# A gap of 128 instead of 64 bytes ahead of four SBUF tiles: y_hi, y_lo, hid_hi and hid_lo

## The chip, the cores and the metric

One Trainium2 chip, one core in use. The time is the device time of one launch in microseconds (us), and the metric is the median of the runs. Engines are named as in the profile: PE is TensorE's matmuls, PEld its weight loads, ACT ScalarE, DVE VectorE, POOL GpSimd, SP the queue that issues the DMAs.

## What is computed

A block of two sub-layers over x of shape (8, 1024, 256) in float32, each behind a layer norm and a residual addition:

```
# first sub-layer, x normalized, D=256, inner width 512, state 16
xz = x @ w_in;  xp, z = split(xz)
xc = silu(causal_conv4(xp) + conv_b)
h  = 0.9*h + 0.1*(xc_t @ w_B);  ys_t = h @ w_C        # scan over the sequence
x  = x + (ys * silu(z)) @ w_out
# second sub-layer, x normalized; 2 of 8 experts for each sequence, by its first token
h  = gelu(x @ W1[e] + b1[e]);   o = h @ W2[e] + b2[e]
x  = x + (o of expert 1 + o of expert 2) / 2
```

## The kernel before

The work goes by chunks of 512 tokens: 16 chunks, two for each sequence. The matmuls take float32r operands. For precision every product A·B is made of three: each operand is split into a high part and the rest (`..._hi`, `..._lo`), and hi·hi, hi·lo and lo·hi are added up in PSUM. ScalarE writes the high parts, VectorE or GpSimd the low parts.

The two operands that this change is about are stationary ones. `y_hi` and `y_lo` hold the gated output ys·silu(z), `hid_hi` and `hid_lo` the GELU rows; all four are [128, 4, 512] in float32, 8192 bytes in each partition. In `tokens` (L1311 to L1313; for the last half chunk `down_tile`, L1320 to L1322) a block of 128 of their columns is loaded as weights, and 256 columns of `w_out_hi`/`w_out_lo` or `w2_hi`/`w2_lo` stream through it:

```
mm(dst, his[:, j, rows], whi, ...)      # L1311
mm(dst, his[:, j, rows], wlo, ...)      # L1312
mm(dst, los[:, j, rows], whi, ...)      # L1313
```

`out_proj` makes 48 of these matmuls for a chunk, `down` another 48. All other products (`project`, L1202 to L1207, for the in-projection and the experts' first layer; `state_in`, L1351 and L1354; `state_out`, L1373) load 128 columns of a weight matrix and stream 512 columns of tokens.

Each engine runs a program written out by hand, with semaphores between them. A step s works on three chunks at once: TensorE makes `xp` of chunk s, `out_proj` of chunk s-1, `z` of chunk s, `up` of chunk s-2, `state_in` of s, half and more of `down` of s-2, `state_out` of s, and the rest of `down`. A step has 84 matmuls of 512 columns and 96 of 256 columns. Steps 4 to 13 are a loop of pairs; an even step also chooses the experts of a sequence. `state_out` waits for VectorE's `state_lo` (L793, tile `state_mix`), which in VectorE's program stands behind `hidden_lo` (L793, tile `hid_lo`) and the scan (L958).

Tiles lie in SBUF in the order in which they are declared, each rounded up to 32 bytes. In this order the padding tiles `to_line`, `wb_rest` and `behind_columns` set the places. From `ident` on, every tile ahead of `behind_columns` starts at a multiple of 512 bytes in its partition, all other operands of matmuls among them, but for the small ones of the router (`first_tok`, `w_router`, `w_spread`). `behind_columns` is read and written by nothing; it is 64 bytes long, so the four tiles behind it start 64 bytes past a multiple of 512. Every block of weights that is loaded from them starts at the same place, since `rows` steps by 512 bytes and `j` by 2048.

Of the kernel before, what the change touches and what calls it, by code (L numbers as in the profile page):

```python
# [11 lines left out]
P = 128  # L12
# [9 lines left out]
def build_block(nc, x, w_in, conv_w, conv_b, w_B, w_C, w_out, Wr, br, W1, b1, W2, b2, out):  # L22
# [19 lines left out]
    with ExitStack() as ctx:  # L42
        def sb(name, shape, dt=F32):
            return ctx.enter_context(nc.sbuf_tensor(name, shape, dt))
# [48 lines left out]
        w1_hi, w1_lo = sb("w1_hi", [P, TOP_K, KD * D], F32R), sb("w1_lo", [P, TOP_K, KD * D], F32R)  # L93
        b_mix = sb("b_mix", [P, JD, P], F32R)
        c_mix = sb("c_mix", [P, DI], F32R)
        behind_columns = sb("behind_columns", [P, 16])
        y_hi, y_lo = sb("y_hi", [P, JD, CH], F32R), sb("y_lo", [P, JD, CH], F32R)
        hid_hi, hid_lo = sb("hid_hi", [P, JF, CH], F32R), sb("hid_lo", [P, JF, CH], F32R)

# [1404 lines left out]
```

## Time and profile before

| | us |
|---|---|
| median of 3 runs | 520.37 |
| the three runs | 520.37, 517.02, 520.53 |
| the profiled execution, its own time | 517.04 |
| its span, first to last instruction | 515.2 |
| PE busy in the span | 508.1 |
| DVE busy | 454.0 |
| ACT busy | 400.0 |
| POOL busy | 342.7 |

The span and all rows come from the one profiled execution; 1.8 us of its own time lie outside the span. Busy is the time in which at least one instruction of the engine runs. Matmuls overlap: each has a duration of some 280 or 390 ns in the profile, and the next starts before it ends, so the pace of TensorE is read from the distance of the starts, not from the durations.

### The profile page before, as it was taken

The numbers are of one execution on the slowest core, as the hardware profiler recorded it, in microseconds if no ns is written. First come the engines' busy times: TensorE is split into PE (matmuls) and PEld (weight loads), VectorE is DVE, ScalarE is ACT, GpSimd is POOL, SyncE is SP. The second block draws the span as 40 slices with busy tenths as digits, with TensorE's granted clock in tenths as the row PEclk, the third lists the DMA queues.
The fourth block names the chain that finished last, engine by engine and source line by source line (L and its number), as shares of the span: only waits on it lengthen the run. The fifth ranks groups of instructions, "written<-read, shape, count | busy, mean of one in ns | idle before, by whom it ended". The sixth has DMA issues, their size and how long they took to land.

```text
span 515.2 us, 9745 instructions
## 1 busy us (share of the span) xinstructions
PE 508.1 (99%) x3008; PEld 447.3 (87%) x3008; DVE 454.0 (88%) x901; ACT 400.0 (78%) x690; POOL 342.7 (67%) x368
## 2 busy tenths in 40 slices
PE   8999999999999999999999999999999999999997
PEld 7788798889898898988889898888988889898987
DVE  5999999999998899989999899998999979896773
ACT  3975877887878788697886979779788787969444
POOL 4764656929875496937969199681996639773381
PEclk9999999999999999999999999999999999999999
DMA  8960104426143352504325161442604333130102
GB/s 247 289 224 1 41 1 144 143 80 208 43 157 89 125 162 78 182 25 166 119 99 186 41 200 45 142 143 68 218 14 149 122 123 122 49 116 0 43 2 81
DMA packets 53922, 57.79 MB, mean 112 GB/s; under 512 B 8714, under 2 KB 50186, under 8 KB 53770
## 3 DMA queue, kind: packets, MB, share of 16 engines
q1 hardware_dynamic: 52042, 57.19, 33.5%
q10 hardware_dynamic: 1856, 0.31, 0.3%
q8 instruction: 12, 0.20, 0.2%
q14 instruction: 12, 0.10, 0.1%
HBM read 35.98 MB, written 21.50 MB: 112 GB/s over the span
## 4 chain that ended last, share of the span: by engine, by line
PE 55%; DVE 14%; issue 9%; ACT 4%; DVEq 0%; POOL 0%; ACTq 0%
PE blk L1202 9%; PE blk L1203 9%; PE blk L1207 9%; PE tok L1311 7%; PE tok L1313 7%; PE tok L1312 7%; DVE hid_lo L793 3%; DVE conv L909 3%; PE blk L1373 3%; PE turn L1351 1%; PE turn L1354 1%; DVE stats_t L830 1%; DVE stats_t L804 1%; DVE normed L892 1%; DVE xn_lo L793 1%
## 5 line engine op out<-in xcount | busy, mean ns | idle before, releaser
L456 POOL TENSOR_TENSOR y_lo<-gate,y_hi 128x512 fp32r<-128x512 f32 x55 | 70.2, 1306 | 105.5 <-ACT y_hi L556 105.5
L909 DVE SCALAR_TENSOR_TENSOR conv<-blk,tap_w,conv 128x512 f32<-128x512 f32 x192 | 130.1, 740 | 11.1 <-ACT conv L618 11.0
L1202 PE MATMUL blk<-xn_hi,w_in_hi 128*128 128x512 f32 x232 | 91.2, 393 | 0.6 <-ACT xn_hi L556 0.6
L1203 PE MATMUL blk<-xn_hi,w_in_lo 128*128 128x512 f32 x232 | 90.6, 391 | 0.0
L421 POOL TENSOR_TENSOR xc_lo<-conv,xc_hi 128x512 fp32r<-128x512 f32 x59 | 71.0, 1221 | 10.5 <-ACT xc_hi L556 10.3
L1311 PE MATMUL tok<-w_out_hi,y_hi 128*128 128x256 f32 x256 | 72.3, 282 | 0.6 <-DVE y_lo L793 0.3
L1207 PE MATMUL blk<-xn_lo,w_in_hi 128*128 128x512 f32 x232 | 72.0, 391 | 0.1
L1313 PE MATMUL tok<-w_out_hi,y_lo 128*128 128x256 f32 x256 | 71.8, 280 | 0.0
L1312 PE MATMUL tok<-w_out_lo,y_hi 128*128 128x256 f32 x256 | 71.8, 280 | 0.0
L618 ACT ACTIVATE conv<-blk,tap_b,tap_w 128x512 f32<-128x512 f32 x64 | 49.1, 778 | 28.3 <-PE blk L1207 24.8
L1311 PE MATMUL tok<-w_hi,hid_hi 128*128 128x256 f32 x248 | 70.2, 283 | 0.3 <-DVE hid_lo L793 0.3
L1313 PE MATMUL tok<-w_hi,hid_lo 128*128 128x256 f32 x248 | 69.6, 281 | 0.0
L1312 PE MATMUL tok<-w_lo,hid_hi 128*128 128x256 f32 x248 | 69.5, 280 | 0.0
L793 DVE TENSOR_TENSOR hid_lo<-hid,hid_hi 128x512 fp32r<-128x512 f32 x64 | 50.8, 820 | 18.4 <-ACT hid_hi L556 18.3
L624 ACT ACTIVATE conv<-conv 128x512 f32<-128x512 f32 x64 | 39.2, 631 | 33.6 <-DVE conv L909 32.6
L464 POOL TENSOR_TENSOR x_mid<-x_mid,b_sel 128x256 f32<-128x256 f32 x60 | 50.8, 882 | 3.2 <-DVE hid_lo L793 1.3
L1207 PEld LDWEIGHTS blk<-xn_lo,w_in_hi 128*128 128x128 f32 x232 | 43.5, 188 | 10.3 <-DVE xn_lo L793 1.1
L1202 PEld LDWEIGHTS blk<-xn_hi,w_in_hi 128*128 128x128 f32 x232 | 43.5, 188 | 9.2 <-DVE w_in_lo L793 0.8
L1203 PEld LDWEIGHTS blk<-xn_hi,w_in_lo 128*128 128x128 f32 x232 | 43.6, 188 | 8.2
L1311 PEld LDWEIGHTS tok<-w_out_hi,y_hi 128*128 128x128 f32 x256 | 48.1, 188 | 1.9 <-issue 0.7
L1312 PEld LDWEIGHTS tok<-w_out_lo,y_hi 128*128 128x128 f32 x256 | 48.9, 191 | 0.5
L1312 PEld LDWEIGHTS tok<-w_lo,hid_hi 128*128 128x128 f32 x248 | 47.4, 191 | 1.1
(175 smaller groups left out, 1300.5 us busy)
## 6 DMA issues: line engine op xcount, KB each, us to landing
spill<-normed SPq DMA_DIRECT2D x25, 512.0 KB, 2.8
normed<-spill SPq DMA_DIRECT2D x100, 128.0 KB, 2.8
x_mid<-in_L_attn_x SPq DMA_DIRECT2D x30, 256.0 KB, 2.7
out<-x_mid SPq DMA_DIRECT2D x30, 256.0 KB, 2.5
x_in<-in_L_attn_x SPq DMA_DIRECT2D x14, 512.0 KB, 3.9
w_all<-in_L_ffn_W SPq DMA_DIRECT2D x2, 2048.0 KB, 12.0
b_all<-in_L_ffn_b SPq DMA_DIRECT2D x1, 1024.0 KB, 14.6
gate<-in_L_attn_w_in SPq DMA_DIRECT2D x2, 256.0 KB, 4.6
```

The costliest lines, as they stand in the source:

```text
L421: nc.gpsimd.tensor_tensor(xc_lo[:, j, :], conv[:, j, 0:CH], xc_hi[:, j, :].bitcast(F32), ALU.subtract).then_inc(xc_lo_set, 1)
L456: nc.gpsimd.tensor_tensor(y_lo[:, j, :], gate_of(o, j), y_hi[:, j, :].bitcast(F32), ALU.subtract).then_inc(y_lo_set, 1)
L464: ins = nc.gpsimd.tensor_tensor(mid(f, q)[:, n, :], mid(f, q)[:, n, :], b2_sel[:], ALU.add)
L618: nc.scalar.activation(conv[:, j, HALO:HALO + CH], blk[j][:], ACT.Identity, bias=tap_b[:, j:j + 1], scale=tap_w[:, j, 0:1]).then_inc(tap_f ...
L793: return nc.vector.tensor_tensor(dst, src, hi.bitcast(F32), ALU.subtract)
L909: nc.vector.scalar_tensor_tensor(cols, blk[j][:], tap_w[:, j, t:t + 1], cols, ALU.mult, ALU.add).then_inc(tap_added, 1)
L1202: mm(dst, whi(k), his(k), start=(k == 0), stop=False)
L1203: mm(dst, wlo(k), his(k), start=False, stop=False)
L1207: ins = mm(dst, whi(k), los(k), start=False, stop=(k == KD - 1))
L1311: mm(dst, his[:, j, rows], whi, start=(j == 0 and n == 0), stop=False, skip_group_check=True)
L1312: mm(dst, his[:, j, rows], wlo, start=False, stop=False, skip_group_check=True)
L1313: ins = mm(dst, los[:, j, rows], whi, start=False, stop=(last and n == 1), skip_group_check=True)
```

## The change

The padding tile doubles, from 16 to 32 float32 elements in each partition. The four tiles behind it move up by 64 bytes, to 128 bytes past a multiple of 512. No instruction is added, removed or reordered.

```diff
         b_mix = sb("b_mix", [P, JD, P], F32R)
         c_mix = sb("c_mix", [P, DI], F32R)
-        behind_columns = sb("behind_columns", [P, 16])
+        behind_columns = sb("behind_columns", [P, 32])
         y_hi, y_lo = sb("y_hi", [P, JD, CH], F32R), sb("y_lo", [P, JD, CH], F32R)
         hid_hi, hid_lo = sb("hid_hi", [P, JF, CH], F32R), sb("hid_lo", [P, JF, CH], F32R)
```

## Rows read from the trace of the kernel before

**Rows 1.** The page: busy time, and TensorE's granted clock in 40 slices.

```profile
PE 508.1 (99%) x3008; PEld 447.3 (87%) x3008; DVE 454.0 (88%) x901; ACT 400.0 (78%) x690; POOL 342.7 (67%) x368
PEclk9999999999999999999999999999999999999999
```

**Rows 2.** Busy time of each engine by stretches of one step (length, busy, instructions).

```profile
118.40:149.20 30.80, 30.61 (x181) 27.00 (x180) 29.11 (x54) 25.82 (x45) 25.68 (x27) 1.00 0.36 120
149.20:180.00 30.80, 30.80 (x186) 27.28 (x185) 27.06 (x58) 24.69 (x41) 18.04 (x20) 1.00 0.37 121
...
sum 154.00, PE 153.66 PEld 135.93 DVE 141.76 ACT 126.88 POOL 113.20; mean PE 30.73 PEld 27.18 DVE 28.35 ACT 25.38 POOL 22.64
```

**Rows 3.** All waits of PEld between 118 and 420 us.

```profile
PEld blk L1373 <- DVE state_mix L793: 1.5, 5, 0.4
```

**Rows 4.** Timeline of PE, a stretch of 48 in step 4, first four and last.

```profile
118.42 0.28 PE L1311 MATMUL tok<-w_out_hi,y_hi 128*128 128x256 f32 x1
118.54 0.28 PE L1312 MATMUL tok<-w_out_lo,y_hi 128*128 128x256 f32 x1
118.66 0.28 PE L1313 MATMUL tok<-w_out_hi,y_lo 128*128 128x256 f32 x1
118.78 0.28 PE L1311 MATMUL tok<-w_out_hi,y_hi 128*128 128x256 f32 x1
...
123.96 0.28 PE L1313 MATMUL tok<-w_out_hi,y_lo 128*128 128x256 f32 x1
124.08 0.40 PE L1202 MATMUL blk<-xn_hi,w_in_hi 128*128 128x512 f32 x1
```

**Rows 5.** Timeline of PE, the first stretch of 48, after a wait.

```profile
43.61 0.36 PE L1311 MATMUL tok<-w_out_hi,y_hi 128*128 128x256 f32 x1 [0.34 <-DVE y_lo L793]
...
44.38 0.28 PE L1311 MATMUL tok<-w_out_hi,y_hi 128*128 128x256 f32 x1
...
49.03 0.28 PE L1313 MATMUL tok<-w_out_hi,y_lo 128*128 128x256 f32 x1
```

**Rows 6.** One line's loads and matmuls: duration in ns, min/median/max.

```profile
L1312 PEld LDWEIGHTS tok<-w_out_lo,y_hi x256: 187/192/192, 43.7 to 488.2; 128*128 128x128 f32 x128
L1312 PEld LDWEIGHTS tok<-w_lo,hid_hi x248: 187/192/192, 74.2 to 509.3; 128*128 128x128 f32 x124
L1311 PEld LDWEIGHTS tok<-w_out_hi,y_hi x256: 186/188/192, 43.6 to 488.1; 128*128 128x128 f32 x128
```

**Rows 7.** Timeline of PE, `project` later in the same step.

```profile
125.46 0.39 PE L1202 MATMUL blk<-xn_hi,w_in_hi 128*128 128x512 f32 x1
...
126.82 0.39 PE L1202 MATMUL blk<-xn_hi,w_in_hi 128*128 128x512 f32 x1
```

**Rows 8.** Timeline of PE around `state_out` in step 4.

```profile
140.99 0.28 PE L1313 MATMUL tok<-w_hi,hid_lo 128*128 128x256 f32 x1
141.46 1.21 PE L1373 MATMUL blk<-state_mix,c_mix 128*128 128x512 f32 x4 [0.19 <-DVE state_mix L793]
```

**Rows 9.** All waits of DVE for others between 190 and 440 us, the longest.

```profile
DVE hid_lo L793 <- ACT hid_hi L556: 6.0, 12, 0.6
DVE conv L909 <- ACT conv L618: 5.9, 16, 0.6
DVE state_mix L793 <- ACT state_mix L556: 4.6, 8, 0.6
```

**Rows 10.** One line each of ACT, DVE and POOL: duration in ns, min/median/max.

```profile
L556 ACT ACTIVATE y_hi<-gate x60: 622/632/639, 39.1 to 482.3; 128x512 fp32r<-128x512 f32 x60
L556 ACT ACTIVATE state_mix<-state x16: 632/632/639, 34.1 to 477.1; 128x512 fp32r<-128x512 f32 x16
L793 DVE TENSOR_TENSOR hid_lo<-hid,hid_hi x64: 644/693/1411, 69.4 to 508.1; 128x512 fp32r<-128x512 f32 x64
L793 DVE TENSOR_TENSOR xn_lo<-normed,xn_hi x50: 676/692/1712, 95.0 to 465.4; 128x512 fp32r<-128x512 f32 x50
L456 POOL TENSOR_TENSOR y_lo<-gate,y_hi x55: 1285/1295/1827, 39.8 to 481.2; 128x512 fp32r<-128x512 f32 x55
L421 POOL TENSOR_TENSOR xc_lo<-conv,xc_hi x59: 1077/1287/1564, 21.9 to 467.0; 128x512 fp32r<-128x512 f32 x59
```

## The prediction

> **What bounds the kernel now.** I read the page first. TensorE is busy 508.1 of 515.2 us, VectorE 454.0, and the clock is at its upper level in every slice [rows 1]. So the clock can neither be lost nor won by a change that moves no work. The table by steps says the same of the inside: of a step of 30.8 us TensorE is busy 30.6 to 30.8, VectorE 29.1 in an even and 27.1 in an odd step [rows 2]. The list of waits has just one kind for the weight loads in ten steps, on VectorE's `state_mix`: 1.5 us in five places [rows 3]. TensorE is the bound, and what one of its instructions loses or gains is seen in the time, but VectorE is close behind in every second step.
>
> A busy engine isn't one at its best pace, so next comes the distance of the starts. This is the view on which everything below rests. In step 4 the 48 matmuls of `out_proj` start from 118.42 to 123.96 us: 5.54 us by 47 distances is 117.8 ns [rows 4]. In the opening the same 48 instructions follow a wait for `y_lo`, and from the seventh on (44.38 us) to the last (49.03) there are 41 distances in 4.65 us: 113.4 ns [rows 5]. Same tiles, same addresses, same clock, and 4.4 ns apart. In the slower stretch the weight load of L1312 takes longer than its neighbours: its median is 192 ns, that of L1311 188 [rows 6]. `project`, whose operands all start at multiples of 512 bytes, makes six matmuls of 512 columns in 126.82 - 125.46 = 1.36 us, 227 ns each, which is twice 113.4 [rows 7]. I read that as two floors with the same price for a column, 0.443 ns, and a surcharge of 4.4 ns for each matmul of 256 columns in most stretches.
>
> How many matmuls carry the surcharge? There are 1536 of the kind (16 chunks by 96). Counted through the timeline between the first (43.61 us) and the last (510 us) of them, 1489 distances lie within a stretch; 1276 are 117 to 119 ns, as in [rows 4], 186 are 113 to 116, as in [rows 5], and 27 are longer. All stretches that TensorE enters without a pause run at 117.8; the faster pace comes only behind a pause, and lasts to the end of the stretch. So the surcharge is 1276 by 4.4 ns = 5.6 us of the kernel.
>
> **The change part by part.** It adds and removes no instruction and moves no wait. What can change is how long an instruction takes that touches one of the four tiles. There are three kinds.
>
> *The writers and readers on ScalarE, VectorE and GpSimd.* Their tiles lie 64 bytes off now, and the trace has twins whose output lies at a multiple of 512: ScalarE 632 ns against 632, VectorE 693 against 692, GpSimd 1295 against 1287 [rows 10]. An offset of 64 costs 0 to 8 ns. For one of 128 the trace has only GpSimd's and ScalarE's source `conv`, which is no worse. Bounds: 8 ns either way by 64 on VectorE is 0.5 us, by 55 on GpSimd 0.4 us. GpSimd's part is hidden, as it is busy 113.2 of 154 us [rows 2]; VectorE's stands in the chain to `state_mix` only in even steps. I take zero, and 0.5 us for the range.
>
> *The DMAs.* None reads or writes the four tiles. Zero.
>
> *The weight loads, 1536 of them, and the matmuls beside which they run.* No row shows another offset of a weight than 0 and 64, so the cost has to be bounded by the nearest rows. Below: the surcharge goes everywhere, -5.6 us, as in [rows 5]. Further below lies only a price never seen in the trace: if 256 columns took 256 cycles at 2.4 GHz, 106.7 ns, then 11.1 ns by 1489 is -16.5 us; I give that little weight, as `project` at offset 0 doesn't reach it either [rows 7]. Above: the surcharge is 13.3 ns for a group of three, and one load of the three (L1312) shows it. If two of three carry it, the pace is 122.2 ns: 1276 by 4.4 and 186 by 8.8 is +7.2 us. If all three do, 126.6 ns: +13.7 us. That is the upper bound.
>
> Which value? The surcharge comes and goes at one and the same address, with the way in which the stretch was entered. So it isn't a price of the address itself but of how loads and matmuls fall into step, and the floor of 0.443 ns for a column is the same for weights at 0 (`project`) and at 64 (the stretch behind the wait). That speaks for a floor that an offset doesn't touch, and for a stepping that it may touch. I take 0 for the forecast, since the two offsets that the trace has, 0 and 64, share a floor. The entries to the stretches stay the same too: `project` ahead, no pause.
>
> On ports the Trainium skill ("TensorE: Matmul & The Clock Gate", step ① of "Step-by-step: what each phase is for") says that TensorE reads the streaming operand and the weights over two independent ports, so that a load takes nothing from the matmul that runs. By that rule an offset changes nothing and the sum is 0. The trace agrees only in part: the same addresses run at 113.4 and at 117.8 ns, so something between the two streams isn't independent. The same page ("Back-to-back issue gap") gives N/2.4 + 2.5 ns for isolated matmuls, an estimate of 109 ns for 256 columns; by it at most 13 us would be to be had, and no stretch of this trace gets there.
>
> *What a gain would meet.* In step 4 the stretch of `down` ahead of `state_out` ran at the faster pace in its second half and ended at 140.99 us; the next matmul started at 141.46, since `state_mix` wasn't ready [rows 8]. That is 0.47 us against 0.11, so 0.36 us of waiting, in one of two steps. VectorE in an even step is busy 29.1 of 30.8 us, and waits for ScalarE some 16.5 us in all over 250 us, 2 us a step [rows 2, 9]. So a gain in an even step is partly handed back at `state_out`. A gain of 4.4 ns by 96 is 0.42 us for a step; I let even steps keep half, odd ones all: 4.2 of the 5.6 us. A loss meets no such cushion: the waits that could take it up are 1.5 us in all [rows 3], and the loss arrives in full but for that.
>
> **The sum.** The profiled execution took 517.04 us, span 515.2. The change as I take it is 0, so a like execution would take 517.0. The median of the runs is 520.37, though, with one run at 517.02 and two near 520.5. The profiled one is at the lower of these levels, and I know no reason for the difference. An unchanged kernel would give a median at one of the two or between; I put it at 519.5.
>
> **The rivals.**
>
> *The surcharge goes (faster).* The loads fall into step with the matmuls in every stretch. For it: the pace exists in the trace with these instructions. Against: one has to believe that 64 more bytes do what a pause does now. It gives 519.5 - 4.2 = 515.3, and 519.5 - 5.6 = 513.9 if VectorE gives nothing back. By the measure of 1% (5.2 us, about what a measurement of this kernel tells from no change) this is on the edge. With luck in the floor too, it reaches 510 and less.
>
> *A second load of each three collides (slower).* Its place is the stretches of L1311 to L1313, its price 4.4 ns more for each matmul, and it decides as soon as more than one load in three is slowed: then the 1489 distances cost +7.2 us, 526.7, and with all three +13.7, 533.2. For it: one load in three does collide at 64, so the streams aren't free of each other, and TensorE has no pause in which to hide a loss. Against: `project` at offset 0 shows no lasting surcharge, so a collision isn't what an arbitrary offset brings.
>
> *The placement doesn't do anything measurable, as the two streams settle into the same pace.* This is the forecast. That the change doesn't move the tiles at all is excluded by the layout: 64 bytes more in front of the four tiles are 64 bytes for each.
>
> **How the numbers follow.** Forecast, same pace: 0.45, between 516.5 and 521. Surcharge gone: 0.25, of which a good half comes out past 1% (515.2); a lower floor: 0.05. More loads collide: 0.25, from 524 to 533, and nearly all past 1% (525.6). That gives faster 0.22, same 0.48, slower 0.30, with some weight on slower because nothing takes up a loss. The range leaves out the lower floor and the worst of the collisions, and takes in the 0.5 us for VectorE: 511.5 to 529.5. The likeliest case alone has 516.5 to 521.
>
> **What the profile of the changed kernel would show.** If the forecast holds: 48 starts of `out_proj` in 5.54 us, L1312's loads at a median of 192 ns, the waits on `state_mix` near 1.5 us in ten steps. If the surcharge is gone: 5.33 us for the 48, loads at 188, and more waiting on `state_mix` in even steps. If more collides: 5.74 us or more for the 48, loads over 188 ns in two lines or three, and no waits of PEld at all. `project` should keep 227 ns in each case, and the durations of ScalarE, VectorE and GpSimd on the four tiles should stay within 8 ns. I would be wrong in kind if `project` changed its pace, if one of the other engines' instructions did, or if the paces stayed and the time didn't.

## The result: 0.43% slower

The changed kernel takes 519.67 us, the median of 20 runs, and the kernel before 517.17 us in 20 runs. The ratio estimated from all of these runs is 1.0043, with an interval of 1.0023 to 1.0062. That is a small loss, and it is real. The median is next to the forecast of 519.5, and inside the range. But the forecast stood for "same pace, no change", counted from a median of 520.4 of three runs. Against the 517.2 of twenty runs there is a change, and the prediction didn't see it coming.

Both kernels have two levels of time. Before: 11 runs at 516.9 to 517.2 and 9 at 520.3 to 520.8. After: 12 at 519.2 to 519.8 and 8 at 522.6 to 523.3. Lower against lower, the change costs 519.4 - 517.1 = 2.3 us. The profiled execution of the changed kernel took 522.59 us, so it is one of the upper level, while that of before is one of the lower. What sets the levels is told below; rows of after are read here with that in mind.

No instruction changed its place or count, so the first view is the busy time. TensorE went from 508.1 [rows 1] to 511.6 us:

```profile
PE 511.6 (98%) x3008; PEld 449.8 (86%) x3008; DVE 457.7 (88%) x901; ACT 400.4 (77%) x690; POOL 341.6 (66%) x368
PEclk9999999999999999999999999999999999999999
```

The timeline of PE in step 4, the first three and the last but one of the 48 matmuls of `out_proj`, and the loads' durations by line (min/median/max, in ns):

```profile
121.67 0.29 PE L1311 MATMUL tok<-w_out_hi,y_hi 128*128 128x256 f32 x1
121.79 0.28 PE L1312 MATMUL tok<-w_out_lo,y_hi 128*128 128x256 f32 x1
121.91 0.28 PE L1313 MATMUL tok<-w_out_hi,y_lo 128*128 128x256 f32 x1
...
127.19 0.28 PE L1312 MATMUL tok<-w_out_lo,y_hi 128*128 128x256 f32 x1
```

```profile
L1311 PEld LDWEIGHTS tok<-w_out_hi,y_hi x256: 186/190/190, 43.6 to 493.5; 128*128 128x128 f32 x128
L1312 PEld LDWEIGHTS tok<-w_out_lo,y_hi x256: 187/188/192, 43.7 to 493.6; 128*128 128x128 f32 x128
L1313 PEld LDWEIGHTS tok<-w_out_hi,y_lo x256: 187/189/191, 43.8 to 493.7; 128*128 128x128 f32 x128
```

From the first start to the 47th there are 46 distances in 5.52 us, 120.0 ns each; before it was 117.8 [rows 4]. The loads of L1312, at 192 before, are at 188 now, and those of L1311 and L1313 are at 190 and 189 [rows 6]. Added up over a group of three, the mean loads take as long as before, 566.7 ns against 566.8, while the pace is slower: the durations of the loads don't measure the surcharge. p1_offsets below shows the same more sharply. Behind a pause the pace isn't 113.4 any more [rows 5] but 118.6: the first stretch of 48 starts at 43.65 and the 43 distances from 44.08 to 49.18 take 5.10 us. Added up over the 1474 distances under 150 ns that each of the two traces has, the 256-column matmuls take 176.5 us against 172.9: the pace costs 3.6 us. So the loss is in the stretches in which the slower rival looked for it. What has to be explained is why 64 bytes do this, and why 2.3 us arrive and not 3.6.

The step lengths answer half of the second. These are the first starts of `out_proj` in steps 8, 9 and 10, from the timeline of PE; first before, then after:

```profile
241.69 0.28 PE L1311 MATMUL tok<-w_out_hi,y_hi 128*128 128x256 f32 x1
...
272.43 0.28 PE L1311 MATMUL tok<-w_out_hi,y_hi 128*128 128x256 f32 x1
...
303.23 0.28 PE L1311 MATMUL tok<-w_out_hi,y_hi 128*128 128x256 f32 x1
```

```profile
245.86 0.29 PE L1311 MATMUL tok<-w_out_hi,y_hi 128*128 128x256 f32 x1
...
276.59 0.29 PE L1311 MATMUL tok<-w_out_hi,y_hi 128*128 128x256 f32 x1
...
307.62 0.29 PE L1311 MATMUL tok<-w_out_hi,y_hi 128*128 128x256 f32 x1
```

An even step took 30.74 us and takes 30.73. An odd one took 30.80 and takes 31.03, 0.23 more, where 96 matmuls by 2.3 ns are 0.22. This pattern repeats through the loop.

### The profile page after: what moved, and what is told of

Read it like the earlier page. It is cut to its first block, busy times and chain, and to the rows that moved or that the text cites. A ratio compares the mean times of both kernels' runs of the same rounds, so it can differ in the third digit from the quotient of the medians.

```text
span 520.8 us, 9745 instructions
## 1 busy us (share of the span) xinstructions
PE 511.6 (98%) x3008; PEld 449.8 (86%) x3008; DVE 457.7 (88%) x901; ACT 400.4 (77%) x690; POOL 341.6 (66%) x368
## 4 chain that ended last, share of the span: by engine, by line
PE 72%; DVE 4%; issue 2%; ACT 1%; DVEq 0%; ACTq 0%
PE blk L1202 12%; PE blk L1207 12%; PE blk L1203 12%; PE tok L1311 9%; PE tok L1313 9%; PE tok L1312 9%; PE blk L1373 2%; PE turn L1354 2%; PE turn L1351 2%; DVE hid_lo L793 1%; ACT hid L663 1%; DVE conv L909 1%; DVE stats_t L804 1%; ACT hid_hi L556 0%; DVE normed L888 0%
## 5 line engine op out<-in xcount | busy, mean ns | idle before, releaser
L456 POOL TENSOR_TENSOR y_lo<-gate,y_hi 128x512 fp32r<-128x512 f32 x55 | 70.1, 1308 | 107.3 <-ACT y_hi L556 107.3
L1311 PE MATMUL tok<-w_out_hi,y_hi 128*128 128x256 f32 x256 | 72.4, 283 | 0.6 <-DVE y_lo L793 0.4
L1313 PE MATMUL tok<-w_out_hi,y_lo 128*128 128x256 f32 x256 | 72.8, 284 | 0.0
L1312 PE MATMUL tok<-w_out_lo,y_hi 128*128 128x256 f32 x256 | 72.6, 284 | 0.0
L1311 PE MATMUL tok<-w_hi,hid_hi 128*128 128x256 f32 x248 | 70.4, 284 | 1.1 <-DVE hid_lo L793 1.0
L1313 PE MATMUL tok<-w_hi,hid_lo 128*128 128x256 f32 x248 | 70.4, 284 | 0.0
L1312 PE MATMUL tok<-w_lo,hid_hi 128*128 128x256 f32 x248 | 70.2, 283 | 0.0
L464 POOL TENSOR_TENSOR x_mid<-x_mid,b_sel 128x256 f32<-128x256 f32 x60 | 49.8, 863 | 3.2 <-DVE hid_lo L793 1.3
L1311 PEld LDWEIGHTS tok<-w_out_hi,y_hi 128*128 128x128 f32 x256 | 48.5, 190 | 1.8 <-issue 0.7
L1311 PEld LDWEIGHTS tok<-w_hi,hid_hi 128*128 128x128 f32 x248 | 46.9, 189 | 3.2 <-issue 1.2
L1312 PEld LDWEIGHTS tok<-w_out_lo,y_hi 128*128 128x128 f32 x256 | 48.2, 188 | 0.6
```

What stands on the lines that cost most here:

```text
L456: nc.gpsimd.tensor_tensor(y_lo[:, j, :], gate_of(o, j), y_hi[:, j, :].bitcast(F32), ALU.subtract).then_inc(y_lo_set, 1)
L464: ins = nc.gpsimd.tensor_tensor(mid(f, q)[:, n, :], mid(f, q)[:, n, :], b2_sel[:], ALU.add)
L1311: mm(dst, his[:, j, rows], whi, start=(j == 0 and n == 0), stop=False, skip_group_check=True)
L1312: mm(dst, his[:, j, rows], wlo, start=False, stop=False, skip_group_check=True)
L1313: ins = mm(dst, los[:, j, rows], whi, start=False, stop=(last and n == 1), skip_group_check=True)
```

## Experiments: which placement makes which pace

I set three theories against each other. R: what counts is the distance in SBUF from the streamed operand to the weights. W: what counts is the place of the weights. N: the pace depends on the other engines' accesses to the moved tiles. The kernels p1_offsets, p2_both and p3_grid hold only TensorE's pattern, so that many placements fit into one run:

```python
CASES = [(place of weights, place of streamed operand, pause), ...]
for w, m, pause in CASES:
    ins = project()              # 24 matmuls of 512 columns, all at multiples of 512 bytes
    if pause: ...                # TensorE waits for ScalarE once
    ins = stretch(w, m)          # 48 matmuls as in tokens: hi.hi, hi.lo, lo.hi
```

**p1_offsets.** 

> This kernel leaves out the whole computation. It holds only TensorE's pattern: 24 matmuls of 512 columns (weights and streamed operand at multiples of 512 bytes), then 48 matmuls of 256 columns in the order hi.hi, hi.lo, lo.hi as in the kernel, with the weights at 0, 32, 64, ... 480 bytes behind a multiple of 512 and the streamed operand at 0; each place once directly behind the 24 and once behind a pause. No other engine works meanwhile. If the pace is made by the two streams of TensorE alone (theories R and W below), the stretch at 64 shows 117.8 ns a matmul (113.4 behind a pause) and the one at 128 120.1 ns (118.8 behind a pause), as in the traces of the two kernels. Theory N (the pace depends on other engines' accesses to the moved tiles) expects one pace, near 113.4, for all places. On the table of the 16 places neither R nor W commits itself; a period shorter than 512 bytes in it would show the size of the unit that collides.

Measured, mean of the last 30 distances in ns:

```
weights at (bytes)      0     32     64     96    128    160    192    224
directly            120.0  118.3  117.8  117.3  120.0  120.0  117.8  116.5
behind a pause      120.0  118.5  117.8  117.3  118.7  120.0  117.8  116.5
```

The places 256 to 480 repeat these numbers within 0.2 ns, with one exception: at 320 behind a pause the pace is 113.3, where 64 has 117.8. So the expected 113.4 behind a pause didn't come at 64, though it did at 320. Theory N falls: with no other engine at work in the stretches the pattern has the pace of the full kernels, 117.8 at 64 and 120.0 at 128. The timeline of PE for those two, first and last matmul of each stretch of 48:

```profile
86.56 0.28 PE L94 MATMUL tok<-moving,weights 128*128 128x256 f32 x1
...
92.09 0.28 PE L96 MATMUL tok<-moving,weights 128*128 128x256 f32 x1
...
132.96 0.29 PE L94 MATMUL tok<-moving,weights 128*128 128x256 f32 x1
...
138.60 0.29 PE L96 MATMUL tok<-moving,weights 128*128 128x256 f32 x1
```

5.53 us by 47 is 117.7 ns, 5.64 by 47 is 120.0. Two more things are seen in the table. The pattern repeats after 256 bytes, so "a multiple of 512" is no special place. And offset 0 is as bad as 128.

The loads of this run settle what their durations say. Directly behind the 24 at offset 0 each load takes 192 ns, and the pace is 120.0 (first row). At 192 the pace is 117.8 (next three rows), and at 320 behind a pause it is 113.3 (last three): the loads are within 1 ns of each other.

```profile
L94 PEld LDWEIGHTS tok<-moving,weights x12: 192/192/192, 41.1 to 45.1; 128*128 128x128 f32 x12
L94 PEld LDWEIGHTS tok<-moving,weights x11: 187/187/187, 181.4 to 185.0; 128*128 128x128 f32 x11
L95 PEld LDWEIGHTS tok<-moving,weights x10: 188/188/188, 181.6 to 184.7; 128*128 128x128 f32 x10
L96 PEld LDWEIGHTS tok<-moving,weights x11: 187/188/188, 181.3 to 184.8; 128*128 128x128 f32 x11
L94 PEld LDWEIGHTS tok<-moving,weights x11: 187/188/188, 286.6 to 290.0; 128*128 128x128 f32 x11
L95 PEld LDWEIGHTS tok<-moving,weights x11: 187/188/188, 286.7 to 290.1; 128*128 128x128 f32 x11
L96 PEld LDWEIGHTS tok<-moving,weights x11: 187/188/188, 286.8 to 290.2; 128*128 128x128 f32 x11
```

So a surcharge of 4.5 ns a matmul can be there with no load longer for it, and counting the slow loads of three gives no price.

**p2_both.** 

> The same reduced kernel, without the computation, with both operands moved: weights and streamed operand at (64,0), (64,64), (128,0), (128,64), (128,128), (0,64), (0,128), (0,256), (256,256), (192,128) and others. Theory R (only the distance of weights and streamed operand counts, modulo 512 or less) expects (64,64) and (128,128) and (256,256) to equal (0,0), and (128,64) and (192,128) to equal (64,0) at 117.8 ns. Theory W (the weights' own place counts) expects (128,64) and (128,128) to equal (128,0) at 120.1 ns, and (0,64) to equal (0,0).

```
weights, streamed   (0,0) (64,64) (128,128) (256,256) | (64,0) (128,64) (192,128) | (128,0) (384,256)
ns, directly        120.0  120.0    120.0     120.0   | 117.8   117.8     117.8   |  120.0    120.0
```

Equal distances have equal paces, whatever the places: R holds and W falls. (0,64), a distance of -64 or 192 modulo 256, has 117.8 as (192,0) does. But (96,32), also a distance of 64, ran at 113.3 ns without a pause, and (128,64) did so behind one. So a distance may have two paces, and how the stretch is entered chooses.

**p3_grid.** 

> The reduced kernel, without the computation: all 64 pairs of a distance (0, 32, ... 224 bytes from the streamed operand to the weights) and a place of the streamed operand (0, 32, ... 224), each directly behind the matmuls of 512 columns. Theory R as it stands (distance alone sets the pace) expects the same pace in a row of equal distance, with the exception already seen: two paces are possible at distance 64 (117.8 and 113.3 ns) and 128 (120.0 and 118.7), and the place of the streamed operand decides which one is entered. So at distance 64 I expect 113.3 at places 32 and perhaps others, 117.8 at 0, 64 and 128; at distance 0 always 120.0; at 224 always 116.5. Theory R+ (the entry decides everything) expects 113.3 ns at other distances too for some place.

```
distance \ streamed operand at    0     32     64     96    128    160    192    224
  0                           120.0  120.0  120.0  120.0  120.0  120.0  120.0  120.0
 32                           118.3  118.3  118.3  118.3  118.4  118.4  118.4  118.3
 64                           117.8  113.3  117.8  113.3  117.8  113.3  117.8  117.8
 96                           117.3  117.3  118.7  117.3  117.3  118.7  118.7  117.3
128                           120.0  118.7  120.0  118.7  120.0  118.7  118.7  118.7
160                           120.0  120.0  120.0  120.0  120.0  120.0  120.0  120.0
192                           117.8  113.3  117.8  117.8  117.8  117.8  117.8  117.8
224                           116.5  116.7  116.7  117.8  116.7  117.8  116.7  116.7
```

The distance sets one pace or a choice of few. Strict R failed in more rows than I had expected: 96 has a second pace too (118.7), and 224 isn't always 116.5 but up to 117.8. Only distances 64 and 192 have 113.3 among them, so R+ is right in one other distance. At 0 and 160 all eight places have the same 120.0.

**e_rel**, the full changed kernel with the streamed operands moved along:

```diff
+        ahead_stream = sb("ahead_stream", [P, 16])
         w_out_hi, w_out_lo = sb("w_out_hi", ...)
         w2_hi, w2_lo = sb("w2_hi", ...)
+        behind_stream = sb("behind_stream", [P, 112])
```

> The changed kernel with w_out_hi, w_out_lo, w2_hi and w2_lo (the operands streamed in L1311 to L1313) moved to 64 bytes behind a multiple of 512, all else in place: weights at 128, streamed operand at 64. Theory R: the pace goes back to 117.8 ns (113.4 behind a pause) and the time to that of before, ratio 1.000 within 0.002. Theory W: pace 120.1 ns, ratio 1.0045. Theory N: ratio 1.0045 too.

Ratio 1.0025 (0.9999 to 1.0051), which says little, since 5 of its 10 runs fell on the upper level and only 1 of the 15 runs of before that were taken with them. Its lower level is 517.2 to 517.7 us, that of before here 516.9 to 517.5. The mean of the distances under 150 ns is 117.2 ns (117.3 before, 119.7 after). So undoing the distance undoes the loss, with the four tiles still at 128. R again.

**e_0**, the gap taken out altogether (the line of `behind_columns` deleted). 

> The kernel before without the gap: all operands of matmuls at multiples of 512 bytes. Both R and W say that the place matters and leave the direction open; I expect a pace between 113.4 and 127 ns, so a ratio between 0.99 and 1.03, and that it agrees with the reduced kernel's stretch at place 0. Theory N expects no difference from one of the two kernels (ratio 1.000 or 1.0045).

Ratio 1.0075 (1.0049 to 1.0102), again with half of the runs on the upper level; its lower level is 519.0 to 519.4. Mean distance 119.7 ns, close to the 120.0 that the reduced kernel has for 0. That is the changed kernel's time at another place with the same pace.

**e_224**: `behind_columns` of 56 elements, so the weights are at 224. 

> The kernel before with the weights at 224 bytes behind a multiple of 512 and the streamed operand at 0. The reduced kernel has 116.5 ns there with and without a pause. Theory R: 117.8 to 116.5 is -1.2 ns for 1276 matmuls, 1.6 us, and +3.2 ns for the 186 behind a pause, 0.6 us: net -1.0 us, ratio 0.998. Theory W gives the same here. If the time doesn't follow the pace, ratio 1.000.

Mean distance 116.9 ns, but ratio 1.0000 (0.9988 to 1.0013), lower level 516.6 to 517.2. For the time that is inconclusive: the expected 1 us is at the edge of what can be told. The steps fit, though: the odd ones take 30.72 us instead of 30.80, and the even ones 30.75 as before.

**e_96_32**: weights at 96, streamed operand at 32 (`behind_columns` 24, `ahead_stream` 8, `behind_stream` 120). 

> The kernel before with the weights (y_hi, y_lo, hid_hi, hid_lo) at 96 and the streamed operand (w_out, w2) at 32 bytes behind a multiple of 512: the distance is 64 as before, but the reduced kernel ran this pair at 113.3 ns directly behind the matmuls of 512 columns. If the entry decides the pace in the full kernel as well: 48 starts of out_proj in 5.36 us instead of 5.54, a gain of 0.4 us in a step of which VectorE's state_mix takes a part back in even steps, so 511.5 to 514 us in runs of the lower level, ratio 0.989 to 0.994. If only the distance counts (strict R): 117.8 ns and ratio 1.000. Theory W: something other than before, at 96 bytes.

The pace came: most stretches at 113.3 ns, and the mean of the distances under 150 ns is 114.5 ns instead of 117.3. Over 1474 distances that is 4.2 us (their sum, 167.3 instead of 172.9 us, looks like more because 12 distances fewer are under 150). The time followed only in part and missed the expected 511.5 to 514 us: ratio 0.9973 (0.9962 to 0.9984), 515.7 us, 1.5 us of 4.2. Odd steps are 30.49 us (30.80 before) and even ones 30.80. The list of waits of the weight loads from 118 to 420 us is longer than before [rows 3]:

```profile
PEld blk L1375 <- DVE state_mix L795: 1.9, 5, 0.4
PEld tok L1313 <- DVE hid_lo L795: 0.5, 2, 0.4
```

## Experiments: who holds the even steps

Even steps last 30.7 to 30.8 us at a pace of 114, 118 and 120 ns alike. So something that doesn't depend on the pace ends them. The waits are for VectorE's `state_mix`, so I took work from VectorE first: `light_*` compute the last tap for 16 of 512 columns.

```diff
-                cols = conv[:, j, HALO - t:HALO - t + CH]
-                nc.vector.scalar_tensor_tensor(cols, blk[j][:], ...
+                n = 16 if t == TAPS - 1 else CH
+                cols = conv[:, j, HALO - t:HALO - t + n]
+                nc.vector.scalar_tensor_tensor(cols, blk[j][:, 0:n], ...
```

**light_64.** 

> A reference point for the two below, with the tiles where the kernel before has them (weights at 64, streamed operand at 0). VectorE is relieved: the last tap of the convolution (t = 3) is computed for 16 of 512 columns only, so part of the convolution is left out; GpSimd has the wait of e_yield, so that no run falls on the upper level. Theory V (half of the steps end on VectorE, and there no pace counts) expects that the steps now both end on TensorE, at some 30.3 to 30.5 us instead of 30.75 and 30.80, and about 512 us for the whole. Theory E (what the pace gives or takes is made up by TensorE itself at the borders of its stretches) expects steps of the same length as before, 30.75 and 30.80.

**light_128.** 

> As light_64 (part of the convolution left out), but with the weights at 128. Theory V: both steps of a pair are longer than in light_64 by the pace, 96 x 2.3 = 0.22 us, and the whole by 3.2 to 3.8 us; in the full kernels it was 0.23 us in odd and nothing in even steps, and 2.3 us in all. Theory E: 2.3 us again.

**light_96_32.** 

> As light_64 (part of the convolution left out), but with the weights at 96 and the streamed operand at 32. Theory V: the whole is shorter than light_64 by 5 to 6.5 us (4.4 ns for each of up to 1489 distances); in the full kernel it was 1.5 us. Theory E: 1.5 us again.

Medians of 10 runs each: 515.57, 517.21 and 514.74 us. The loss by 128 is 1.6 us and the gain by 96/32 is 0.8, less than in the full kernels. Taken at their word the expectations of theory V failed, and those of E nearly came. But the even steps weren't freed: 30.86 to 30.93, 30.68 to 30.73 and 31.15 to 31.22 us. The timeline of VectorE in step 8 of light_64 suggests why. The taps end earlier, and what follows has grown:

```profile
243.52 1.03 DVE L912 SCALAR_TENSOR_TENSOR conv<-blk,tap_w,conv 128x512 f32<-128x512 f32 x3
244.52 0.69 DVE L825 TENSOR_TENSOR x_mid<-tok,x_mid 128x512 f32<-128x512 f32 x1
245.71 0.69 DVE L825 TENSOR_TENSOR x_mid<-tok,x_mid 128x512 f32<-128x512 f32 x1 [0.50 <-PE tok L1316]
246.31 3.48 DVE L795 TENSOR_TENSOR xn_lo<-normed,xn_hi 128x512 fp32r<-128x512 f32 x2
```

Two `xn_lo` take 3.48 us, against 2.54 in the kernel before; undisturbed they take 1.3. GpSimd is at work on `xc_lo`, `w_hi` and `w_lo` at that time. In odd steps of the loop one `xn_lo` of the `light_*` kernels even takes 4.5 to 4.8 us. So cutting VectorE's work moved the meeting of the two engines and didn't end it; the work must be taken from GpSimd, with VectorE's program left as it is.

**pool_64.** 

> A reference point for the two below, tiles placed as before (weights at 64, streamed operand at 0), with the wait of e_yield. GpSimd is relieved: from the second sequence on, L431, L439, L442 (the split of the chosen experts' weights) and L464 (b2) work on 16 columns only, so part of the second sub-layer is left out. VectorE's program is untouched. Theory G (even steps end on VectorE because GpSimd stretches VectorE's instructions: xn_lo 1.52 and 1.09 us, hid_lo 1.22 twice, neg_mean 0.80, against 0.69 and 0.3 without company) expects these back at 0.7 us, the waits of TensorE for state_mix gone, even steps at 30.5 us instead of 30.75, odd ones unchanged at 30.80. Theory E (TensorE itself makes up for the pace at the borders of its stretches) expects even steps at 30.75 as before.

**pool_128.** 

> As pool_64 (part of the second sub-layer left out), weights at 128. Theory G: now both steps of a pair are longer than in pool_64 by 96 x 2.3 = 0.22 us, the whole by 3.0 to 3.6 us (2.3 us in the full kernels). Theory E: 2.3 us again, none of it in even steps.

**pool_96_32.** 

> As pool_64 (part of the second sub-layer left out), weights at 96, streamed operand at 32. Theory G: both steps of a pair shorter than in pool_64 by 0.3 to 0.4 us, the whole by 4.5 to 6 us (1.5 us in the full kernel). Theory E: 1.5 us again.

Their edit, at L431, L439, L442 and L464:

```diff
-                    ins = nc.gpsimd.tensor_tensor(mid(f, q)[:, n, :], mid(f, q)[:, n, :], b2_sel[:], ALU.add)
+                    ins = nc.gpsimd.tensor_tensor(mid(f, q)[:, n, 0:16], mid(f, q)[:, n, 0:16], b2_sel[:, 0:16], ALU.add)
 # in all chunks; and 16 columns in the splits of w1 and w2, from the second sequence on
```

Medians 515.18, 518.76 and 511.56 us (5, 8 and 4 runs, none more than 0.5 us off its median). The even steps are 30.42, 30.66 and 30.16 us, the odd ones 30.80, 31.03 and 30.49; no wait of TensorE is left in the list from 118 to 420 us. The loss by 128 is now 3.58 us, for 3.4 us of pace (119.74 against 117.46 ns by 1474): all of it arrives. The gain by 96/32 is 3.62 us, for 4.5 us of pace (114.37 ns). Theory G holds. What theory E said is a small part of it: behind the faster stretches `project` takes 10.94 us in place of 10.91 and 5.50 in place of 5.47, about 0.08 us an even step with the others. The expected 4.5 to 6 us left this out, so that this expectation failed by its size.

VectorE in step 8, first before, then pool_64, both from the timeline of DVE:

```profile
249.67 2.54 DVE L793 TENSOR_TENSOR xn_lo<-normed,xn_hi 128x512 fp32r<-128x512 f32 x2
...
258.38 3.57 DVE L793 TENSOR_TENSOR hid_lo<-hid,hid_hi 128x512 fp32r<-128x512 f32 x4
```

```profile
248.96 1.30 DVE L797 TENSOR_TENSOR xn_lo<-normed,xn_hi 128x512 fp32r<-128x512 f32 x2
...
256.25 1.36 DVE L797 TENSOR_TENSOR hid_lo<-hid,hid_hi 128x512 fp32r<-128x512 f32 x2
258.16 0.69 DVE L797 TENSOR_TENSOR hid_lo<-hid,hid_hi 128x512 fp32r<-128x512 f32 x1 [0.55 <-ACT hid_hi L560]
```

The same two `xn_lo` take 2.54 us beside GpSimd's full work and 1.30 beside the cut one; the `hid_lo` go from 3.57 us for four to 0.69 each.

## Experiments: the two levels, and a version that beats both

The long instruction of the upper level stands in the timeline of DVE of the changed kernel, in step 3, with GpSimd's beside it:

```profile
95.18 5.98 DVE L793 TENSOR_TENSOR xn_lo<-normed,xn_hi 128x512 fp32r<-128x512 f32 x1 [0.70 <-ACT xn_hi L556]
```

```profile
91.06 2.17 POOL L402 TENSOR_SCALAR normed<-x_in,neg_mean,rstd 128x256 f32<-128x256 f32 x4 [0.20 <-issue]
93.19 2.35 POOL L421 TENSOR_TENSOR xc_lo<-conv,xc_hi 128x512 fp32r<-128x512 f32 x2
95.49 2.84 POOL L464 TENSOR_TENSOR x_mid<-x_mid,b_sel 128x256 f32<-128x256 f32 x4
98.28 2.33 POOL L421 TENSOR_TENSOR xc_lo<-conv,xc_hi 128x512 fp32r<-128x512 f32 x2
```

GpSimd works without a gap from 91.1 to 100.6 us, and the VectorE instruction that started at 95.2 ends at 101.2. In the profile of before, which is of the lower level, it took 0.92 us. The time of the level is lost right there: e_rel (upper) and before (lower) have nearly the same pace, and from the first start of `out_proj` in step 3 to that of step 4 e_rel takes 34.31 us against 31.34, in step 4 31.30 against 30.92; together 3.35 us, and no other step differs by more than 0.1.

**e_yield**, the kernel before with one wait more:

```diff
                     if has_attn(s):
                         split_conv(a, (0, 1))
+                    if isinstance(s, int) and s == 3:
+                        pool.wait_ge(t2_lo, f * KD + 1)
                     add_b2(f, 1, half - 1)
```

> This one is about the two levels of the time, 517.1 and 520.4 us, that both kernels show from run to run. The kernel before, with one wait more: in step 3 GpSimd starts its additions of b2 (L464) only when VectorE has done the first subtraction of turn2_lo (L793, xn_lo). Theory S (starvation): in runs of the upper level this one VectorE instruction takes 6.0 us instead of 0.9, because GpSimd's instructions follow each other without a gap and VectorE's is not let in until they pause at 100.6 us; with the wait GpSimd pauses, the instruction gets in, and all runs lie at 517 to 517.5, none above 519. Theory T (the level has another cause, a DMA or the start of the loop's code, and the long instruction is its sign only): some 2 in 5 runs still lie at 520.5.

11 runs, 516.9 to 517.7, none on the upper level. But of the 24 runs of before taken with them only 1 was, so this alone tells little. The next set of runs tells more: light_64, light_128, light_96_32 and best have the same wait, and of their 42 runs none is on an upper level, while 15 of the 35 runs of before taken with them were. The `light_*` kernels also changed VectorE's work; best, whose work is that of the full kernel, has 0 of 12. In step 3 the long instruction is in the two profiles of the upper level that I have (after and e_rel, 5.98 us each) and in no other. That speaks for theory S. How often the level comes without the wait isn't steady, so a rarer upper level in spite of the wait isn't excluded.

**best**, e_96_32 with that wait. 

> The full kernel with both things that the experiments point to: weights at 96 and streamed operand at 32 bytes behind a multiple of 512, and GpSimd's wait in step 3. From e_96_32 and e_yield I expect all runs at 515.4 to 516.5 us and none near 519, ratio 0.997 to the lower level of before. If the starvation has another place with this pace, some runs lie at 518 to 519.

515.61 us in 12 runs (514.9 to 516.2), none above. The ratio of 0.9945 (0.9923 to 0.9967) has before's upper runs in it; to its lower level of 517.1 us it is 0.997.

**best2**, with one wait more, in even steps:

```diff
                 choose_b2(half - 1, chosen)
+                pool.wait_ge(g_lo, f * JF + JF)
                 add_b2(f, 0, half - 1)
```

> The full kernel once more, nothing left out: weights at 96, streamed operand at 32, the wait in step 3, and in even steps GpSimd starts its additions of b2 (L464) only when VectorE has done its four hid_lo. Theory G: the two hid_lo that took 1.22 us take 0.69, state_mix is ready 0.5 to 1 us earlier, and even steps shrink from 30.80 to 30.3 or so; over some six even steps 2 to 3.5 us, so 512 to 513.5 us, ratio 0.990 to 0.993. If the additions now delay something else (state_mix or the end of the step), nothing is gained: 515.5.

512.35 us (512.1 to 512.5, 4 runs), ratio 0.9903 (0.9887 to 0.9920) to before, all of whose 12 runs taken with them are of the lower level. The four `hid_lo` take 2.48 us instead of 3.57, and in place of best's five waits of the loads between 118 and 420 us there is one:

```profile
256.81 2.48 DVE L798 TENSOR_TENSOR hid_lo<-hid,hid_hi 128x512 fp32r<-128x512 f32 x4
```

```profile
PEld blk L1378 <- DVE state_mix L798: 0.3, 1, 0.3
```

Even steps are 30.16 us from step 6 on, odd ones 30.49: they are as long as those of pool_96_32, where no wait is left. The placement gave 1.5 us by itself, and with GpSimd's two waits added it is 4.9 us. The wait in even steps alone, at the old placement, wasn't run.

## Why the prediction was wrong, step by step

**The bound and the view.** TensorE as the bound and the distance of starts as the view proved right. The surcharge itself did too, but not that one load of three carries it: the loads' durations don't follow the pace (p1_offsets). What was to stay did stay: `project` remained at 227 ns, and GpSimd's `y_lo` and VectorE's `hid_lo` nearly kept theirs, at 1308 and 810 ns in the mean against 1306 and 820.

**The step that failed: "I take 0 for the forecast, since the two offsets that the trace has, 0 and 64, share a floor."** The row for offset 0 was `project`, of 512 columns, and the row for 64 a stretch of 256 columns. Divided by columns they agree, 0.443 ns, and I took this for the same floor. The reduced kernel has 256-column matmuls at distance 0: 120.0 ns, the worst value of the table, and the full one (e_0) 119.7. For 128, the offset that was asked about, the runs show 120.0 and 119.7, a surcharge of 2.4 ns over before, where I put 0. With 512 columns at distance 0 the same reduced kernel has 226.7 ns, twice 113.3, and nothing of it shows. A load takes 187 to 192 ns, longer than the 113 to 120 between two starts of 256 columns and shorter than the 227 of 512; whether that is the reason no run shows. The row that I compared said nothing of the case asked about. From there the conclusion that the pace "isn't a price of the address itself" went wrong as well. Both are true: the distance sets which paces exist (117.8 and 113.3 at 64; 120.0 and 118.7 at 128), and the entry chooses between them.

**The slower rival** had the right place and direction: the stretches of L1311 to L1313 run slower. What it counted, the slow loads of three, isn't what makes the price, so its size was off. I doubled the surcharge to 122.2 ns and +7.2 us; the pace rose to 120.0, half a surcharge more, which is 3.6 us with what was lost behind pauses.

**"A loss meets no such cushion."** It met one, though no larger than the sentence goes on to allow, "1.5 us in all": 3.6 us of pace gave 2.3 us, and the 1.3 us that are missing are about the waits of [rows 3], which fell from 1.5 to 0.6 us. But the prices of this rival, 526.7 and 533.2, took nothing off for them. An even step of before had 0.33 us to spare (30.75 us, and 30.42 in pool_64), so it took up the 0.24 us of the slower pace whole. What I overlooked is that a chain on VectorE that needs 30.74 us hides whatever TensorE needs less than that, in a gain as in a loss. The same step priced a gain at 4.2 of 5.6 us; e_96_32 gave 1.5 of 4.2. I had let an even step keep half of it, and it kept nothing: VectorE's stretch from the first tap to `state_mix` isn't shortened by a faster `out_proj`. The two rows that say so were quoted, VectorE at 29.1 of 30.8 us and TensorE waiting at 141.46 [rows 2, 8], and weighed too lightly.

**The level.** I put an unchanged kernel between two levels for which I had no reason. Twenty runs put before at 517.2, and the changed kernel lies 2.3 us above it for a reason that the forecast had put at nothing. That 519.5 is next to 519.67 is luck.

## What to carry to other kernels

Where a stretch of short matmuls loads new weights for each, read the distance of the starts against other stretches of the same shape: here several paces for one form of instruction came from the distance in SBUF between the loaded and the streamed tile and from the entry, and that distance is worth a sweep in a reduced kernel, which costs one run for 64 placements. Don't read the price from the durations of the loads. Don't carry a pace from one matmul width to another. And compare the lengths of alternating steps before and after: if one kind moves and the other stands, the other has a different owner, and a gain must be bought there first.

## What the hardware showed that I hadn't expected

- The pace of load and matmul pairs of 128 and 256 columns in float32r depends on the distance of the two operands in SBUF with a period of 256 bytes: 116.5 to 120.0 ns, and 113.3 with some entries at 64 and 192. The Trainium skill ("TensorE: Matmul & The Clock Gate", step ① of "Step-by-step: what each phase is for") says that the two read ports are independent and a load takes nothing from the running matmul. No other engine was at work in the stretches of p1_offsets, and the pace moved by 3.5 ns with the distance alone, so for this form the two aren't independent. What collides stays open.
- A VectorE instruction that takes 0.68 us undisturbed took 5.98 while GpSimd finished one instruction and ran six more without a gap. The levels of the whole are 3.3 us apart, in both kernels. The Trainium skill ("SBUF — State Buffer", "SBUF: two separate sides") has a pair of ports that one of the two holds for a whole instruction while the other blocks. The trace agrees on the blocking, but not on one instruction as its length: VectorE's stayed out while GpSimd began six instructions one after the other.
- How often the upper level comes differs between sets of runs of the same kernel: 9 of 20, 15 of 35, but 1 of 15, 1 of 24 and 0 of 12 for the kernel before. It may differ between kernels too: beside that 1 of 15, e_rel had 5 of 10 and e_0 3 of 6. A median over few runs is mostly a draw between the levels.
